# A decoder layer with routed experts: list writes placed one step later on GpSimd, and fewer waits in TensorE's expert loop

## The reference

```python
x = x + attention(layernorm(x))                  # 16 heads, one shared key/value head, 4 rows of 512 tokens
x = x + ssm(ctx_1024, layernorm(x))              # state space scan, 16 states
h = layernorm(x)                                 # 2048 tokens, 512 wide
probs = softmax(h @ gate_weight.T)               # 32 experts
topv, topi = top_k(probs, 8)                     # weights under 0.05 are dropped, the rest renormalised
for e in range(32):                              # gate_up 512 -> 2*192, down 192 -> 512
    g, u = split(h @ w_gu[e].T)
    acc += (silu(g) * u) @ w_d[e].T * combine[:, e]
return x + acc
```

## Time and profile before

| | |
|---|---|
| median of three runs | 1494.35 us |
| the profiled execution | 1485.55 us |
| its span, first to last instruction | 1483.7 us |
| mean granted TensorE clock | 0.950 |
| busy share: TensorE, VectorE, ScalarE, GpSimd | 89%, 75%, 63%, 31% |
| DMA of entries into lists (L2840) | 128, mean 1537 ns |
| additions into the output (L2949) | 68, mean 1656 ns |
| w_hi, xt_hi matmuls (L1156) | 272, that is 68 blocks of four |

### The profile page before, as it was taken

One profiled execution on the slowest core, in us unless ns is written; L12 is line 12 of the kernel. 1 busy time (PEld: TensorE's weight loads), 2 busy tenths in 40 slices (PEclk: granted clock), 3 DMA queues, 4 the chain that ended last, 5 costly groups with the idle time before them and its releaser, 6 DMA issues.

```text
span 1483.7 us, 26467 instructions
## 1 busy us (share of the span) xinstructions
PE 1326.2 (89%) x6890; PEld 1021.6 (69%) x6891; DVE 1117.6 (75%) x1545; ACT 936.8 (63%) x2450; POOL 466.5 (31%) x367
## 2 busy tenths in 40 slices
PE   4699999999999999999999899998931689999996
PEld 4378885548898554889855488985421578888885
DVE  4488599959888994988899498887775347776763
ACT  4668885368878546887853688784230347666663
POOL 0001001000044211134421103461404675666664
PEclk9889999999999999999999999999965789999998
DMA  7449988632687953268796326868721369999983
GB/s 276 194 129 276 270 207 235 159 108 65 167 239 175 241 148 108 63 167 244 169 241 155 102 60 165 254 155 204 172 93 43 82 161 229 226 236 235 223 194 53
DMA packets 137517, 256.81 MB, mean 173 GB/s; under 512 B 48718, under 2 KB 50207, under 8 KB 129105
## 3 DMA queue, kind: packets, MB, share of 16 engines
q0 software_dynamic: 36480, 122.30, 36.8%
q1 hardware_dynamic: 76704, 86.70, 20.0%
q10 hardware_dynamic: 24240, 46.68, 10.0%
HBM read 166.37 MB, written 46.21 MB: 143 GB/s over the span
## 4 chain that ended last, share of the span: by engine, by line
PE 55%; DVE 13%; issue 10%; DMA 9%; ACT 5%; POOL 4%; another core or an unknown queue 1%; SPq 0%; POOLq 0%; ACTq 0%; DVEq 0%
PE bank L665 9%; PE bank L688 7%; DMA y<-dbu 4%; POOL lists L2840 4%; PE pair L537 4%; PE bank L1156 3%; PE bank L537 3%; PE bank L1157 3%; PE bank L1158 3%; PE pair L614 3%; PE pair L616 3%; PE pair L615 3%; PE bank L650 2%; PE bank L652 2%; PE bank L651 2%
## 5 line engine op out<-in xcount | busy, mean ns | idle before, releaser
L665 PE MATMUL bank<-v_aug,probs 128*128 128x129 f32 x2048 | 247.9, 277 | 6.3 <-ACT probs L1344 6.3
L665 PEld LDWEIGHTS bank<-v_aug,probs 128*128 128x128 f32 x2048 | 241.8, 193 | 15.3 <-ACT probs L1344 10.8
L2840 POOL DMA_INDIRECT lists<-entry,slot x128 | 196.7, 1537 | 136.1 <-DVE slot L2314 98.4
L688 PE MATMUL bank<-wout,o_t 128*128 128x512 f32 x512 | 231.2, 606 | 8.8 <-DMA wout<-in_wout 4.5
L1344 ACT ACTIVATE probs<-bank 128x512 f32<-128x512 f32 x256 | 152.5, 603 | 67.1 <-PE bank L665 36.1
L688 PEld LDWEIGHTS bank<-wout,o_t 128*128 128x128 f32 x512 | 98.0, 195 | 129.5 <-issue 125.0
L1353 ACT ACTIVATE decay<-delta,neg_a 128x511 f32<-128x511 f32 x256 | 164.3, 722 | 26.1 <-DVE state L2138 18.9
L2138 DVE TENSOR_TENSOR_SCAN dbu<-decay,dbu 128x1024 f32<-128x1024 f32 x64 | 144.7, 2283 | 3.2 <-ACT decay L1353 1.3
L2138 DVE TENSOR_TENSOR_SCAN state<-decay,state 128x1024 f32<-128x1024 f32 x64 | 144.5, 2281 | 1.3
L2949 POOL DMA_INDIRECT out<-y_ring,add_ids x68 | 112.6, 1656 | 79.9 <-ACT y_ring L1912 37.0
L2855 POOL DMA_DIRECT2D y<-dbu x32 | 29.2, 913 | 297.0 <-DVE dbu L2143 240.4
(11 more groups left out here) (238 smaller groups left out, 2906.1 us busy)
## 6 DMA issues: line engine op xcount, KB each, us to landing
y<-dbu POOLq DMA_DIRECT2D x32, 1024.0 KB
w_raw<-in_w_exp ACTq DMA_DIRECT2D x64, 512.0 KB
wq<-wq_dram POOLq DMA_DIRECT2D x30, 1024.0 KB
y<-state POOLq DMA_DIRECT2D x28, 1024.0 KB
wout<-in_wout SPq DMA_DIRECT2D x64, 256.0 KB, 5.6
b_bc<-bc_dram SPq DMA_DIRECT2D x64, 256.0 KB
c_bc<-bc_dram SPq DMA_DIRECT2D x64, 256.0 KB
lists<-in_const ACTq DMA_DIRECT2D x3, 2904.0 KB, 20.7
```

The costliest lines, as they stand in the source:

```text
L665: mm = pe.matmul(bank_o[half][:, (t % 2) * (DH + 1):(t % 2 + 1) * (DH + 1)], probs[:, k, t * P:(t + 1) * P], v_aug[:, k, :], start=(k == 0 ...
L688: mm = pe.matmul((bank_o + bank_s)[t][:], o_t[:, h, t * P:(t + 1) * P], wout[:, h % 4, :], start=(h == 0), stop=(h == H - 1))
L2840: pool.indirect_dma_start(out=lists, out_offset=bass.IndirectOffsetOnAxis(ap=slot[:, t, k:k + 1].bitcast(U32), axis=0), in_=entry[:, t, :] ...
```

## The change

On GpSimd each group of sends from 2 on moves one place back: 0 and 1 stand ahead of gets 0 and 1, group 2 ahead of gets 2 and 3, group 3 ahead of gets 4 and 5, and groups 4, 5, 6, 7 stand one at each of the first four pairs of the loop. On TensorE `gate_up` no longer waits for `wlo_ok`; one wait for the weights of experts 0 and 1 stands ahead of the first block, and the later ones are implied, since VectorE splits an expert's weights ahead of the tokens that `xtlo_ok` tells of. `down` no longer waits for `yb_ok`, which ScalarE's order implies (`weigh` stands ahead of the next `ht`). The wait for the addition moves from ahead of the first down matmul to ahead of the fifth.

```diff
             def gate_up(blk, e, parity):
                 hi, lo = gate_up_w(w_hi, e), gate_up_w(w_lo, e)
-                pe.wait_ge(S["wlo_ok"], e * 3 + 3)
                 pe.wait_ge(S["xtlo_ok"], blk + 1)
...
-            def down(blk, e):
+            def down(blk, e, q, r):
                 hi, lo = down_w(w_hi, e), down_w(w_lo, e)
                 pe.wait_ge(S["htlo_ok"], blk + 1)
-                pe.wait_ge(S["yb_ok"], blk)
...
                 pe.matmul(y_bank[:], ht_hi[:, P:], hi[:, 1, :], start=False, stop=False)
+
+                wait_apart(pe, S[f"added{r % 2}"], q * 32 + (ADDED0 + (r // 2 - 1) * 16))
                 pe.matmul(y_bank[:], ht_lo[:, P:], hi[:, 1, :], start=False, stop=True).then_inc(S["y_ps"], 1)
...
-                    wait_apart(pe, S[f"added{r % 2}"], q * 32 + (ADDED0 + (r // 2 - 1) * 16))
-                    down(blk, es[r])
+                    down(blk, es[r], q, r)
...
             xt(0, 0)
+            pe.wait_ge(S["wlo_ok"], 2 * 3)
             gate_up(0, first, 0)
...
-            send_last(range(0, 3))
+            send_last(range(0, 2))
...
             for r in range(QUAD):
-                if r % MIN_BLK == 0 and r > 0:
-                    send_last(range(r // MIN_BLK + 2, r // MIN_BLK + 3))
+                if r == MIN_BLK:
+                    send_last(range(2, 3))
                 pool.wait_ge(S[f"get_in{r}"], 32)
                 get(r)
-            send_last(range(4, 5))
+            send_last(range(3, 4))
...
-                    k = q * 2 + r // 2 + 5
-                    if k < TOPK:
-                        send_last(range(k, k + 1))
+                    k = q * 2 + r // 2 + 4
+                    send_last(range(k, k + 1))
                     get_next(q, r)
```

## The result

| | before | after |
|---|---|---|
| median | 1491.26 us (20 runs) | 1500.12 us (20 runs) |
| range | 1480.37 to 1499.84 | 1489.47 to 1510.23 |
| the profiled execution | 1485.55 us | 1494.49 us |

The ratio after to before is 1.0066, interval 1.0043 to 1.0089: the change costs some 10 us. The forecast was 1491 us, 3.2 us under a median of 1494.35 us taken from three runs; over 20 runs that median is 1491.26 us. Within 0.5% of no change had a chance of 0.62 there; the measured change is 0.66%. The measured time lies in the range given, but the kernel moved the other way. A ratio compares only runs within 1.5% of their kernel's fastest, which in e1 to e4 leaves out 7 of the 35 runs of the kernel before and none of the experiments', so that the ratio of e1, 1.0052, would be 1.0031 by the means of all runs (1.0001 to 1.0061 by two standard errors).

A forecast was written before the change was run, and what follows sets the result against it. TensorE and VectorE were taken to set the pace, with GpSimd's additions following at a fixed distance. Sends 0, gate_up -3.2, down 0: -3.2 us off the median gave 1491 us; range 1483 to 1507 us.

The forecast's parts named there:

- Sends in front, 0: GpSimd before the first get: without four sends it idles longer, and the first get starts when it did; 0 us.
- the 1.4 us kept for the range: SyncE's chain before the first get: two 0.70 us steps, perhaps slow because of the sends, might go; 1.4 us gain.
- A fourth group in the loop delays block 9 by 5.0 us: GpSimd, loop's fourth pair: a new group of sends costing 5.73 us makes block 9's addition about 5.0 us later.
- Its lateness 5.9 us: Block 9's addition on GpSimd: would come 5.9 us after its weighing, against 0.87 us in the profile.
- Caught up at 1 us a pair, 0 at the end: GpSimd's additions: lateness shrinks from 5.9 to 2.9 us in three or four pairs; cost at the end 0.
- The bound that I had named: GpSimd's additions: landing at 5.9 us of lateness may be as slow as at 0.87 us; then nothing is caught up.
- The first rival: From block 6 on, additions carry the delay to the end: 1499 us, or 1508 with 0.3 us a pair slip; chance 0.31.
- two prices of a transfer: Landing of GpSimd's additions: 5.7 to 8.2 us by the rows, 2.6 us by the skill's estimate, which was not relied on.
- gate_up, -3.2 us: TensorE's gate_up: the removed wait saves about 0.1 us once per expert, 32 times; -3.2 us, bounds 0 and 6.4.
- two-block time of 8.52 us: Sign of being right, on VectorE: its time for two blocks goes from 8.62 to about 8.52 us.
- The moved wait, 0 with 3.4 us from above: TensorE's down, between fourth and fifth matmul: some 0.2 us of sequencer time, hidden, so 0; unhidden 0.2 x 17 = 3.4 us.
- The cover that I named: TensorE: hidden transposes wait 0.26 us for VectorE anyway, hiding the up to 0.2 us delay from the moved wait.

The follow-up runs named there:

- e1: Kernel before with only GpSimd's moved sends from the change, TensorE's loop as before; ratio 1.0052 to the kernel before.
- e4: Kernel before with only the addition's wait moved from ahead of the first to ahead of the fifth down matmul; ratio 1.0013.
- e5: Kernel before, unchanged, run again for a second trace; ratio 0.9995.
- e7: Kernel before with sends moved a further step on: group 0 alone in front, groups 3 to 7 at the loop's first five pairs; ratio 1.0369.
- e11: Kernel before with only send groups 6 and 7 in the loop, waits for wlo_ok and yb_ok gone, register loads in mid-expert; ratio 1.0006.
- e14: Kernel before with the first weight part's load halved (256 of 512 KB) from the fifth expert on; ratio 1.0007.
- e17: Second trace of the kernel before with the first weight part's load halved from the fifth expert on; span ends 357.6 us after the first send.
- e3: Kernel before with TensorE's waits for wlo_ok and yb_ok gone, addition's wait and sends as before; ratio 0.9981.
- e15: Kernel before with only send groups 6 and 7 in the loop, waits for wlo_ok and yb_ok gone, six useless ScalarE copies; ratio 0.9903, median 1479.76 us.
- e6: Kernel before with 12 useless copies (7.5 us) on ScalarE after the third expert; ratio 0.9929.
- e2: Kernel before with only TensorE's part of the change: two waits gone, addition's wait ahead of the fifth down matmul; ratio 1.0022.
- e9: Kernel before with VectorE's and ScalarE's register load of the next block count moved to the middle of the expert; ratio 1.0057.
- e13: Changed kernel with 28 useless copies (17 us) on ScalarE after the third expert; ratio 1.0013 to the kernel before.

## Why the prediction failed, step by step

- **Sends in front, 0: right.** Get 0 started 17.69 us after the first send, 18.94 in the profile before, but 17.52 and 17.65 in its other traces. Nothing was gained; the 1.4 us kept for the range are not there.
- **A fourth group in the loop delays block 9 by 5.0 us: nearly right in size, 5.9.** With the old sends block 9 is added 92.7 to 95.5 us after the first send in the traces without ScalarE's stops, with the new ones at 97.5 to 100.6 (means 93.6 of nine and 99.5 of six): 5.9 us.
- **Its lateness 5.9 us: wrong, 11.8.** The working took 0.87 us as the start. In that execution ScalarE had been stopped, TensorE's side was late and GpSimd looked on time. Usually the lateness is 6.0 to 6.9 us with the old sends, and 5.9 on top of that is what was measured. The tokens were indeed short: TensorE waits 19.9 us for them in 6 places, in e5 16.9 in 4.
- **Caught up at 1 us a pair, 0 at the end: wrong, and the step that failed.** The term for the sends was put at nothing by a rule from three rows, all 0.87 to 4.38 us late; e1 measured 7.8 us for it. At 6 us of lateness a pair takes 8.95 to 9.08 us and at 8.7 us 9.66, so a late chain as a rule does not catch up, it keeps TensorE back. The three rows were also a poor sample of the landing. In 16 traces (all but e7, e11, e14 and e17; blocks 11 to 59, second additions, from the semaphores' updates) it took 5.8 us on average at 2 to 3.2 us of lateness, 5.4 at 3.2 to 4, 6.0 at 5.8 to 7 and 6.6 from 8 up: at most a slight fall, and then a rise. The bound that I had named, that nothing is caught up, was near the true case, though the landing at 6 us is not as slow as the 7.3 us of block 9. The first rival, with its chance of 0.31, is in essence what happened. The measured 10 us lie between its 5.0 and its 13.7 us; that its 1499 us stands so near 1500.12 is partly luck, since the median it starts from was 3.1 us too high. Its rule "0.3 us a pair lost" is also near (9.05 - 8.65 = 0.4), only that the kernel before mostly pays it as well. Of the two prices of a transfer weighed there, neither the rows nor the estimate of the Trainium skill (DMA: Bandwidth & Descriptors, "Anatomy of one DMA"), 2.6 us, held: at 6 us of lateness additions needed 4.8 to 7.0 us to land in e3's trace. The 5.4 us a pair given there does not follow from its own terms either (1.93 + 2.6 = 4.5).
- **gate_up, -3.2 us: not contradicted.** e3 measured -2.8 us with an interval from -7.9 to +2.2. The two-block time of 8.52 us was not to be seen, since the pace of the additions covers it; e15, with the waits gone, has 8.58 against 8.62 in e6.
- **The moved wait, 0 with 3.4 us from above: the cost is not proven, the mechanism is seen.** e4 measured +1.9 (-3.0 to +6.9), e2 less e3 some 6 us with both intervals overlapping; the transposes behind it are late 12 times, 5.5 us in all, in e2 and once, 0.4 us, in e3. The cover that I named, the 0.26 us before the hidden transposes, exists only while VectorE sets the pace.

A second trace of the kernel before would have shown the error: in neither of its other traces is block 9 on time. Why a late chain is slower stays open: the landing of second additions is 0.3 us longer at the slow pace (6.0 against 5.7 us), which is most of the 0.4 us, but what makes it longer is not shown. Nor is the cause of ScalarE's stops, or of the turns in mid-loop. It wasn't tried to take the additions' DMAs off the weight loads' engines.

## What to carry to other kernels

A profile is one execution. Before a step is priced by how late one engine is against another, look in the waits view for stops that nothing in the program explains (here 21.4 us of "remote"), and ask what the lateness would be without them. A loop in which a chain of DMAs follows the matmuls may have two paces, and a shift of a few us at its start, in either direction, can then be worth 0.4 us in every pair for as long as the pace lasts. A rule that a late chain catches up is to be read at the lateness that the change will bring, not at that of the rows at hand.

## What was not expected of the hardware

- A register load on VectorE took a median of 0.31 us in e9 and of 0.92 us in e5, where most of those over 0.6 us (15 of 19) ended within 0.2 us of the end of GpSimd's issue of an addition.
- ScalarE's 7.5 us of useless copies made the program 0.7% faster (e6), and 17 us of them took most of the change's loss back (e13).
- Two kernels may differ by 9 us in their medians while single executions of each spread over 20 us; the spread is partly the code ahead of the sends (1123.4 to 1144.2 us to the first send of the last row, in 20 traces) and partly when, if at all, the loop changes its pace.
